# One scan in place of a subtraction for the lower half of an LSTM state (one Trainium2 core)

## The reference, cut to what matters

```
def step(carry, xw_t):
    prev_h, prev_c = carry
    a = xw_t + prev_h @ Wh
    i = jax.nn.sigmoid(a[:, :Hdim])
    f = jax.nn.sigmoid(a[:, Hdim:2 * Hdim])
    o = jax.nn.sigmoid(a[:, 2 * Hdim:3 * Hdim])
    g = jnp.tanh(a[:, 3 * Hdim:])
    next_c = f * prev_c + i * g
    next_h = o * jnp.tanh(next_c)
    return ((next_h, next_c), next_h)
```

## Time and profile before

| What | Value |
|---|---|
| Median of 3 runs | 324.32 us (324.11 to 324.44) |
| The profiled execution's own time | 322.7 us |
| Its span in the trace | 320.9 us |
| Granted TensorE clock, mean | 0.899 of full speed |
| Busy: PE, DVE, ACT, POOL | 80%, 70%, 55%, 20% |
| Steps of the recurrence | 128, from 53.9 us to 287.2 us (start of the first and the last `h_hi`) |

### The profile page before, as it was taken

The page is one execution under the profiler, slowest core; times in us unless marked ns, Lnnn a source line. Parts: engine busy times, 40 slices in busy tenths (PEclk is TensorE's granted clock), DMA queues, the critical chain, the costliest instruction groups (busy, mean ns, idle before and its releaser), DMA issues.

```text
span 320.9 us, 8982 instructions
## 1 busy us (share of the span) xinstructions
PE 256.5 (80%) x3353; PEld 157.5 (49%) x3354; DVE 224.6 (70%) x1076; ACT 177.3 (55%) x560; POOL 64.7 (20%) x88
## 2 busy tenths in 40 slices
PE   2618967998988999898898998998888888875435
PEld 1417745665666656565655665554444445332011
DVE  5886895688876767776767777556575564556985
ACT  4328985655756867567535665544225223246850
POOL 3712154930002029600100000001000000003800
PEclk9955975899977899999959999999999999997955
DMA  3424301000001000000000000000000000000003
GB/s 93 105 54 115 61 8 33 3 2 2 5 3 33 2 2 3 3 2 3 2 2 1 5 0 2 3 2 2 0 3 3 0 3 0 2 0 0 3 0 131
DMA packets 7499, 5.59 MB, mean 17 GB/s; under 512 B 1696, under 2 KB 6304, under 8 KB 7456
## 3 DMA queue, kind: packets, MB, share of 16 engines
q1 hardware_dynamic: 7168, 4.89, 6.2%
q10 hardware_dynamic: 288, 0.13, 0.1%
HBM read 2.40 MB, written 1.05 MB: 11 GB/s over the span
## 4 chain that ended last, share of the span: by engine, by line
PE 45%; DVE 28%; ACT 17%; issue 7%; DMA 1%; SPq 0%; DVEq 0%; POOL 0%; ACTq 0%
PE bank L1334 16%; PE bank L1393 7%; ACT tanh_c L993 6%; ACT gates_sb L988 5%; DVE prod L1827 5%; DVE h_hi L1835 5%; DVE gates_sb L1830 4%; PE bank L1253 3%; PE bank L1056 3%; DVE neg_max L1614 2%; PE bank L1194 2%; PE bank L1138 2%; PE bank L1101 1%; PE bank L1248 1%; DVE mods L1919 1%
## 5 line engine op out<-in xcount | busy, mean ns | idle before, releaser
L1393 PE MATMUL bank<-ident_b,zero_w 128*128 128x512 bf16 x272 | 77.4, 384 | 0.0
L988 ACT ACTIVATE gates_sb<-bank 128x64 f32<-128x64 f32 x128 | 28.6, 223 | 64.5 <-PE bank L1334 61.0
L1334 PEld LDWEIGHTS bank<-h_hi,wh_hi 128*128 128x128 f16 x508 | 23.3, 98 | 70.8 <-DVE h_hi L1835 64.6
L1827 DVE SCALAR_TENSOR_TENSOR prod<-gates_sb 128x32 f32<-128x32 f32 x128 | 24.6, 192 | 38.0 <-ACT gates_sb L988 33.8
L1334 PE MATMUL bank<-h_hi,wh_hi 128*128 128x16 f16 x508 | 32.9, 173 | 22.8 <-DVE h_hi L1835 22.0
L993 ACT ACTIVATE tanh_c<-gates_sb 128x16 f32<-128x16 f32 x128 | 27.6, 216 | 41.3 <-DVE gates_sb L1830 38.1
L1835 DVE TENSOR_TENSOR h_hi<-o_scaled,tanh_c 128x16 f16<-128x16 f32 x128 | 22.4, 175 | 25.6 <-ACT tanh_c L993 25.3
L1334 PE MATMUL bank<-h_lo,wh_hi 128*128 128x16 f16 x508 | 32.6, 173 | 0.0
L1393 PEld LDWEIGHTS bank<-ident_b,zero_w 128*128 128x128 bf16 x272 | 22.3, 98 | 20.1 <-issue 9.1
L1334 PE MATMUL bank<-h_hi,wh_lo 128*128 128x16 f16 x508 | 31.1, 169 | 0.0
L1253 PE MATMUL bank<-x1T,wx_sb 128*128 128x128 f32 x128 | 30.9, 330 | 0.0
(11 more groups left out here) (234 smaller groups left out, 446.0 us busy)
## 6 DMA issues: line engine op xcount, KB each, us to landing
xT_sb<-xT SPq DMA_DIRECT2D x4, 256.0 KB, 4.5
v_all<-v_tok SPq DMA_DIRECT2D x16, 64.0 KB, 2.1
outT<-probs SPq DMA_DIRECT2D x3, 256.0 KB, 2.5
v<-v_tok SPq DMA_DIRECT2D x16, 32.0 KB, 1.9
wh_sb<-Wh SPq DMA_DIRECT2D x1, 256.0 KB, 2.9
wx_sb<-Wx SPq DMA_DIRECT2D x1, 256.0 KB, 2.9
outT<-probs SPq DMA_DIRECT2D x2, 128.0 KB, 2.0
ffn_nat<-w_down SPq DMA_DIRECT2D x1, 176.0 KB, 3.4
```

The costliest lines, as they stand in the source:

```text
L988: A.activation(gates_sb[:, now, 0:GATES * B], bank[(t // BANK_STEPS) % 2][:, slot:slot + GATES * B], ACT.Tanh, scale=scale).then_inc(gates ...
L1334: ins = E.matmul(bank[dst][:, col:col + B], w[:, g * P:(g + 1) * P], h[:, part, :], start=False, stop=True, skip_group_check=True)
L1393: E.matmul(bank[1 - ((t + 1) // BANK_STEPS) % 2][:, :], zero_w[:, :], ident_b[:, :].unsqueeze(1).broadcast_to([P, 4, P]), start=False, sto ...
L1827: V.scalar_tensor_tensor(out=prod[:, :], in0=G[:, now, 0:2 * B], scalar=1.0, in1=G[:, now, 3 * B:5 * B], op0=ALU.add, op1=ALU.mult).then_i ...
```

## The change

The lower part is computed by one scan instead of a subtraction. A scan runs along its row and keeps a running value: each element is (gate operand x running value) - second operand. For this the operands lie interleaved in threes: `o_tanh` holds (0, o_scaled, tanh_c) for each batch row, and `h_hi` holds (-1, 0, h_hi). So the three running values of a batch row are 1, o_scaled, and o_scaled x tanh_c - h_hi, and the third is `h_lo`. The scan has 48 elements for the 16 batch rows and needs `h_hi`, but not `hidden`. It therefore stands directly behind `h_hi`, waits for `hidden_hi`, and the f32 product `hidden` is written behind it. `hid_max`, in every eighth step, now waits for `hidden_f` itself. `h_hi`, `h_lo`, `o_scaled` and `tanh_c` are views of every third element: 6 bytes apart for the f16 ones, 12 bytes for the f32 ones. Three memsets at the program's start write the constants.

```
-        o_scaled = sb("o_scaled", [P, B], F32)
-        tanh_c = sb("tanh_c", [P, B], F32)
-        h_hi = sb("h_hi", [P, 2, B], F16)
-        h_lo = sb("h_lo", [P, 2, B], F16)
+        o_tanh_all = sb("o_tanh", [P, B, 3], F32)
+        h_hi_all = sb("h_hi", [P, 2, B, 3], F16)
+        h_lo_all = sb("h_lo", [P, 2, B, 3], F16)
...
+        o_scaled, tanh_c = o_tanh_all[:, :, 1], o_tanh_all[:, :, 2]
+        h_hi, h_lo = h_hi_all[:, :, :, 2], h_lo_all[:, :, :, 2]
...
+            V.memset(o_tanh_all[:, :, 0], 0.0).then_inc(tiny, 1)
+            V.memset(h_hi_all[:, :, :, 0], -1.0).then_inc(tiny, 1)
+            V.memset(h_hi_all[:, :, :, 1], 0.0).then_inc(tiny, 1)
...
-                V.tensor_tensor(h_hi[:, now, :], o_scaled[:, :], tanh_c[:, :], ALU.mult).then_inc(hidden_hi, 1)
-                hs = hidden[:, t * B:(t + 1) * B]
-                V.tensor_tensor(hs, o_scaled[:, :], tanh_c[:, :], ALU.mult).then_inc(hidden_f, 1)
-                v.wait_ge(hidden_f, t + 1)
-                V.tensor_tensor(h_lo[:, now, :], hs, h_hi[:, now, :], ALU.subtract).then_inc(hidden_lo, 1)
+                V.tensor_tensor(h_hi[:, now, :], o_scaled, tanh_c, ALU.mult).then_inc(hidden_hi, 1)
+                v.wait_ge(hidden_hi, t + 1)
+
+                V.tensor_tensor_scan(h_lo_all[:, now, :, :].rearrange("p b k -> p (b k)"), o_tanh_all[:, :, :].rearrange("p b k -> p (b k)"),
+                                     h_hi_all[:, now, :, :].rearrange("p b k -> p (b k)"), 0.0, ALU.mult, ALU.subtract).then_inc(hidden_lo, 1)
+                V.tensor_tensor(hidden[:, t * B:(t + 1) * B], o_scaled, tanh_c, ALU.mult).then_inc(hidden_f, 1)
                 if t % BANK_STEPS == BANK_STEPS - 1:
+                    v.wait_ge(hidden_f, t + 1)
```

More of the change, by code:

```diff
@@ L992, in _ @@
                 ac.wait_ge(cell, t + 1)
-                A.activation(tanh_c[:, :], gates_sb[:, nxt, GATES * B:], ACT.Tanh, scale=0.5).then_inc(tanh_done, 1)
+                A.activation(tanh_c, gates_sb[:, nxt, GATES * B:], ACT.Tanh, scale=0.5).then_inc(tanh_done, 1)
                 if t < LAST_SLOT:
@@ L1831, in _ @@
                                        op0=ALU.mult, op1=ALU.add).then_inc(cell, 1)
-                V.tensor_scalar(o_scaled[:, :], G[:, now, 2 * B:3 * B], 1.0, H_SCALE / 2, ALU.add, ALU.mult).then_inc(o_ready, 1)
+                V.tensor_scalar(o_scaled, G[:, now, 2 * B:3 * B], 1.0, H_SCALE / 2, ALU.add, ALU.mult).then_inc(o_ready, 1)
                 v.wait_ge(tanh_done, t + 1)
                 v.wait_ge(o_ready, t + 1)
-                V.tensor_tensor(h_hi[:, now, :], o_scaled[:, :], tanh_c[:, :], ALU.mult).then_inc(hidden_hi, 1)
-                hs = hidden[:, t * B:(t + 1) * B]
-                V.tensor_tensor(hs, o_scaled[:, :], tanh_c[:, :], ALU.mult).then_inc(hidden_f, 1)
-                v.wait_ge(hidden_f, t + 1)
-                V.tensor_tensor(h_lo[:, now, :], hs, h_hi[:, now, :], ALU.subtract).then_inc(hidden_lo, 1)
+                V.tensor_tensor(h_hi[:, now, :], o_scaled, tanh_c, ALU.mult).then_inc(hidden_hi, 1)
[3 more added lines that the diff above has]
+                V.tensor_tensor(hidden[:, t * B:(t + 1) * B], o_scaled, tanh_c, ALU.mult).then_inc(hidden_f, 1)
                 if t % BANK_STEPS == BANK_STEPS - 1:
+                    v.wait_ge(hidden_f, t + 1)
                     piece = t // BANK_STEPS
```

## The result

The changed kernel takes 333.77 us (median of 4 runs, 332.92 to 337.18) against 324.31 us (324.11 to 324.44). The ratio is 1.031, with a 95% interval of 1.024 to 1.038: slower, as forecast, but by 9.5 us where 1.2 were forecast, and outside the range of 321.5 to 329.0. Its profiled execution took 333.46 us, its span is 331.7 us: 10.8 us over the span before. Its granted clock was 0.861 of full speed against 0.899.

What follows compares the result with a forecast made beforehand. The wait for h_lo was taken to bound most steps, DVE's queue being the second limit. Path -0.4 and queue +1.7 made +1.3, of which +1.2 was kept: 324.3 + 1.2 = 325.5 us, range 321.5 to 329.0.

Steps and rivals of the forecast that it cites:

- The wait for `h_lo` sets 111 of 127 steps.: PE's third group of weight loads waits for h_lo, up to 0.10 us in each of 111 steps.
- The gain of a step is 5 ns: Path to h_lo: about 85 free steps each gain 5 ns, together -0.4 us.
- The scan's two slots an element, 259 ns.: Scan on DVE: two slots of 1.06 ns for each of 48 elements plus 158 ns fixed, 259 ns.
- The first: Rival: scan at the ordinary price, 209 ns, -4.3, 320.0 us; chance 0.15 including all S well under 245.
- the third rival: Scan on DVE costs three slots or more an element, 310 ns: +7, 331.5 us; chance 0.06.
- S: The scan's duration on DVE, taken as 259 ns; the gain of a step is 0.264 - S, at most 0.10.
- DVE's queue, +1.7: Later work behind the scan on DVE costs 0.1 + 0.27 + 1.14 + 0.20 = +1.7 us.
- The steps with one maximum: Some 21 steps with one 512-column maximum on DVE lose about 5 ns each, 0.1 us together.
- I price this at nothing, since the elements stay within 48 neighbours.: Spread operands of o_scaled, the cell's tanh, h_hi and PE's reads cost zero.
- the second rival: Spread operands cost time on h_hi: +1.3, 326.8 us, or +6.8, 332.3 us; chance 0.08.
- its lower price of 0.6 ns an element: Spread operands on h_hi: 16 elements cost 10 ns, x 128 = +1.3, 326.8 us.
- The zero-weight products begin behind the third group and move with it.: PE's zero-weight products follow the third group of weight loads and move with it; no cost was given.

Runs made afterwards that it cites:

- experiment 4: Changed order with packed operands and the scan on constant tiles, with 80 or 16 scan elements instead of 48: 333.37 and 314.27 us, one run each.
- experiment 1: Kernel before with the changed DVE order but packed operands, scan on constant tiles, lower part left out: ratio 1.009, on another chip 1.004.
- experiment 3: Kernel before, with its order and subtraction, but only o_scaled and tanh_c spread 12 bytes apart: 328.3 us, single run.

## Why the prediction was wrong, point by point

- *The wait for `h_lo` sets 111 of 127 steps.* Right in kind; in experiment 4 a scan of 68 ns more or 66 less moved a quiet step by 66 and 68 ns, and about 100 of the 127 steps moved by 55 ns or more each time. The count of 111 itself was not tested.
- *"The gain of a step is 5 ns", -0.4.* It did not show: with packed operands (experiment 1) `h_lo` ended 2 ns earlier, and the last 50 steps took 88.0 us as before.
- *The scan's two slots an element, 259 ns.* Right: 258, and 2.1 ns an element over 16, 48 and 80. The first and the third rival, which rested on S, fall. The Trainium skill's "half throughput" ("DVE: opcode table, instruction layouts, handler registers and perf-mode slots", section "Datapath and trigger behaviour") agrees with the trace: 2.1 ns an element against 1.06. That two operations in sequence are the reason was argued, and no run shows it.
- *DVE's queue, +1.7.* Right in size: 1.4 in ten steps of experiment 1 (forecast 1.4), and 0.2 behind the last step (forecast 0.2). That the ten add up is partly luck: t = 17, 19 and 54 cost 0.07 each and not 0.09, t = 15 and 47 0.19 and 0.20 and not 0.12. The steps with one maximum stayed as long as the quiet ones.
- *"I price this at nothing, since the elements stay within 48 neighbours."* This is a step that failed. Spread operands cost 14 ns on `h_hi` and 7 on the tanh, and with about 5 in PE's part, less 2 that the scan gained, a step is 24 ns longer, +3.1 us. That the 5 come of the spread `h_hi` and `h_lo`, which PE reads, was not tested by itself; with `h_hi` and `h_lo` packed (experiment 3) they are gone. It was the second rival, with 0.08; its lower price of 0.6 ns an element (10 ns on `h_hi`) was near. It missed the tanh, which writes such a view. The page "SBUF — State Buffer" of the Trainium skill, section "Door 1: The DMA port swizzle", says that such strides are free; the trace disagrees (175 to 189 ns), and I let the page lower the rival's chance. The same sentences of the Trainium skill ask for two accesses to a 16-byte line, which f32 elements 12 bytes apart do not have on every line, so I had read it too widely; the f16 ones 6 bytes apart have them and cost 9 ns all the same. The lower of the two rows for spread operands (0.6 ns an element) should have been the central guess for instructions on the path of all 128 steps; measured are 14 / 16 = 0.9 ns an element on `h_hi` and 7 / 16 = 0.4 on the tanh.
- *"The zero-weight products begin behind the third group and move with it."* True of their place and wrong as an account of what they do. They hold the granted clock up: 12 more of them raised it from a range of 0.813 to 0.892 to one of 0.898 to 0.917. The forecast has no term for the clock, though the page before shows its low stretches; this is the other step that failed, and the larger one. PE waits longer in the changed kernel, 24 ns in every step and 0.1 to 0.3 us in the DVE-bound ones. In the profiled run the steps with PE late cost +7.0; on one chip fillers took back 8 of 13 us.
- Sum for the profiled run: spread operands 127 x 0.024 = 3.1; DVE's queue 1.9 less the 24 ns of its 11 steps, 1.6; PE late 7.0 less the 24 ns of its 28 steps, 6.3; two shorter steps -0.5; behind the last step 0.3. Together 10.8, as measured.

What stays open: why the clock falls in one run and not in the next of the same program (325.8 and 334.0 for the layout alone), and how the loss splits between longer steps and DVE-bound ones, since the layout alone and the order alone each brought long low stretches in some runs only, and both together in most. No run separated it further.

## What to carry to other kernels

An instruction on the path of every step of a recurrence is to be priced to the nanosecond, with its layout: a view of every third element cost 3 to 8% of it. Where a kernel has filler work for its clock, an edit that changes step times can change the clock too: here 24 ns more in each step (1.4%) and 0.1 to 0.3 us in eleven of them, 5 us in all, lost 9 to 13 us, and 12 more filler products took back 8 of the 13. So try the fillers again before judging such an edit. And the wait inside PE's burst of products did not appear in the chain of waits; look for the gap between instructions that could follow at once.

## What was not expected of the hardware

- Views with gaps inside 16 bytes are not free: tanh on ACT, 16 elements written 12 bytes apart, 223 ns and not 216; a product on DVE reading two such operands 180 and not 175; writing f16 6 bytes apart 9 more; a subtraction reading and writing f16 6 bytes apart 188 and not 174.
- `hidden`, the same instruction on the same packed operands, takes 168 ns behind `h_hi` (before) and 149 behind the scan (experiment 1): a duration depends on what runs ahead of it.
- The same program on one chip took 329.1 to 340.3 us, with a granted clock of 0.892 in the shortest run and 0.813 in the longest.
